# First attention of a fused layer chain: a new order of projections, maximum rows and value blocks, and inputs of the next batch loaded at other points

## What is computed

```
x = x + attention0(layernorm(x), ctx)     # 16 heads of 64, softmax(q k' / 8) v, then w_out
x = x + experts(layernorm(x))             # two of eight experts
x = x + attention1(layernorm(x), ctx)     # 16 heads of 16
x = x + quantised_ffn(layernorm(x))
```

```
q = layernorm(x) @ w_q;  k, v = split(ctx @ w_kv);  out = softmax(q @ k.T * 64**-0.5) @ v
```

## Time and profile before

| | |
|---|---|
| median of 3 runs | 3297.62 us |
| the profiled execution, its time | 3297.44 us |
| its span, first to last instruction | 3295.6 us |
| mean granted TensorE clock | 0.974 of full speed |
| TensorE matmul busy | 3098.3 us, 94% |
| VectorE busy | 2310.2 us, 70% |
| ScalarE busy | 1630.6 us, 49% |
| GpSimd busy | 1303.7 us, 40% |

### The profile page before, as it was taken

How to read it: one execution, slowest core, us unless ns; L and a number is a source line. 1 busy time by engine, 2 the same in 40 slices (tenths; PEclk the granted TensorE clock), 3 DMA queues, 4 the chain that set the end, 5 groups by cost and what they waited for, 6 DMA issues and landing times. The chain is left out here.

```text
span 3295.6 us, 40332 instructions
## 1 busy us (share of the span) xinstructions
PE 3098.3 (94%) x14204; PEld 1886.0 (57%) x14204; DVE 2310.2 (70%) x3680; ACT 1630.6 (49%) x1850; POOL 1303.7 (40%) x610
## 2 busy tenths in 40 slices
PE   6999999999999999999999969799999999999578
PEld 4556556556556566565565546455555555554368
DVE  5675785675775766757746524688888888888589
ACT  3443443443443434534534412366676576666388
POOL 1764774764765756747746723200000000000102
PEclk9999999999999999999999979799999999999798
DMA  8454553453553453544535332322322323222202
GB/s 219 112 124 110 128 139 89 114 146 85 126 147 83 106 144 99 123 123 107 125 102 121 78 106 80 83 44 65 73 50 66 67 49 72 66 49 59 72 13 90
DMA packets 182475, 317.40 MB, mean 96 GB/s; under 512 B 35081, under 2 KB 94289, under 8 KB 182289
## 3 DMA queue, kind: packets, MB, share of 16 engines
q1 hardware_dynamic: 182288, 315.00, 38.9%
HBM read 92.58 MB, written 29.36 MB: 37 GB/s over the span
## 5 line engine op out<-in xcount | busy, mean ns | idle before, releaser
L900 POOL TENSOR_TENSOR a_prob_sum<-a_prob_sum,a_prob 128x1024 f32<-128x1024 f32 x384 | 924.3, 2407 | 60.5 <-ACT a_prob L620 5.7
L620 ACT ACTIVATE a_prob<-a_t 128x1024 f32<-128x1024 f32 x512 | 516.6, 1025 | 660.5 <-PE a_t L445 472.7
L767 DVE TENSOR_REDUCE a_mhalves<-a_m 128x1 f32<-128x512 f32 x1024 | 690.2, 680 | 115.0 <-PE a_m L409 107.7
L1650 ACT ACTIVATE a_prob<-a_t 128x1024 f32<-128x1024 f32 x512 | 497.2, 1024 | 183.7 <-PE a_t L1491 182.8
L1747 DVE TENSOR_REDUCE a_mhalves<-a_m 128x1 f32<-128x512 f32 x807 | 537.5, 685 | 59.5 <-PE a_m L1470 55.2
L452 PE MATMUL a_o<-a_prob,a_v_all 128*64 128x512 f32 x2048 | 494.2, 605 | 0.0
L409 PE MATMUL a_m<-a_kh_n,a_qz 128*128 128x512 f32 x1024 | 415.0, 417 | 19.3 <-DVE a_kl_n L761 15.0
L900 POOL TENSOR_TENSOR a_prob_sum<-a_prob 128x1024 f32<-128x1024 f32 x64 | 153.3, 2395 | 575.0 <-ACT a_prob L620 511.8
L1470 PE MATMUL a_m<-a_vh,a_qz 128*128 128x512 f32 x807 | 335.7, 436 | 10.5 <-DVE x_sb L1819 4.5
L437 PE MATMUL a_t<-a_q_hl,a_k_hh 128*128 128x512 f32 x1024 | 324.1, 398 | 4.6 <-ACT a_prob L620 4.5
L445 PE MATMUL a_t<-a_q_hm,a_k_lm 66*128 66x512 f32 x1024 | 321.7, 395 | 0.0
(11 more groups left out here) (273 smaller groups left out, 4200.2 us busy)
## 6 DMA issues: line engine op xcount, KB each, us to landing
a_k_hh<-a_kh_n SPq DMA_DIRECT2D x256, 256.0 KB, 4.5
a_k_lm<-a_kl_n SPq DMA_DIRECT2D x128, 256.0 KB, 4.9
a_q_hl<-a_qz SPq DMA_DIRECT2D x128, 128.0 KB, 2.3
a_q_hm<-a_qz SPq DMA_DIRECT2D x128, 128.0 KB, 2.4
a_q_hl<-a_ql_n SPq DMA_DIRECT2D x128, 128.0 KB, 2.4
a_vs<-a_vh SPq DMA_DIRECT2D x256, 64.0 KB, 2.4
a_wq<-wq_parts SPq DMA_DIRECT2D x63, 256.0 KB, 2.7
a_wk<-wk_parts SPq DMA_DIRECT2D x63, 256.0 KB, 3.0
```

Of the source, the lines that this page charges most:

```text
L620: nc.scalar.activation(prob[:, t % RING], ps_t[t % 2][:, :, :], ACT.Exp, scale=SCALE0).then_inc(s_exp, 1)
L767: nc.vector.tensor_reduce(mhalves[:, qt, hd, n:n + 1], ps_m[:, n, :], AX.X, ALU.max).then_inc(s_max, 1)
L900: nc.gpsimd.tensor_tensor(acc, prob[:, (t - 1) % RING] if t == 1 else acc, prob[:, t % RING], ALU.add).then_inc(s_acc, 1)
L1650: nc.scalar.activation(prob[:, t % RB, 2 * j:2 * j + 2, :], ps_t[j][:, :, :], ACT.Exp, scale=SCALE1).then_inc(s_exp, 1)
```

## The change

In the first attention alone:
- On TensorE, `probs_v` of tiles 0 to 3 stand in one block (before: 0, 1, two maxima, 2, 3), and scores 5 come behind it. In p=7 scores 0 come ahead of the first maximum. The last two maxima come directly ahead of the values of tiles 4 and 5, and `max_rows` behind these values (in p=6, where the values 4 to 7 are one block, `max_rows` stays ahead of them).
- `project_k` comes ahead of `project_q`, and on ScalarE and VectorE the keys' splits ahead of the queries' (in p=6 queries stay first). The semaphores `s_kq`, `s_hi`, `s_lo` are split by keys and queries. SP's stacking starts with the keys.
- The reciprocals of the pair before stand ahead of maxima 7, 7, 8, 9 (before: 0, 9, 11, 12).
- The next rows are loaded straight into `xn`, as soon as the transposes have read it, and scaled in place, one row tile in each of p=1 to 4. The next context is loaded at the start of the batch, behind the storing of the context's parts.
- In p=6 VectorE subtracts the low transposed rows between the two parts of the context.

```diff
@@ block.sync, stack
+                sp.wait_ge(s_hk, nx.g + 1)
+                for hd in range(2):
+                    move(k_hh[heads[0], u, hd, :], kh_n[heads[hd], :])
+                    move(k_hh[heads[1], u, hd, :], kh_n[heads[hd], :])
+                sp.wait_ge(s_hq, 2 * nx.g + 2)
                 for hd in range(2):
                     move(q_hl[heads[0], u, hd, :], qz[heads[hd], hd, :])
                     move(q_hm[heads[0], u, hd, :], qz[heads[hd], hd, :])
...
@@ block.sync, batch
                 if not last:
 
-                    sp.wait_ge(s_cl, 2 * (b + 1))
-                    sp.dma_start(x_in[:], x_view[:, bass.ds((b + 1) * QT, QT), :]).then_inc(s_xin, 16)
+                    sp.wait_ge(s_tr, b + 1)
+                    sp.dma_start(xn[:], x_view[:, bass.ds((b + 1) * QT, QT), :]).then_inc(s_xin, 16)
...
+                if not last:
+                    load_context(b + 1)
                 stack(pair(b, 1), pair(b, 2))
...
-                if not last:
-
-                    sp.wait_ge(s_ln, 14 * (b + 2))
-                    load_context(b + 1)
                 stack(pair(b, NP - 1), None if last else pair(b + 1, 0))
@@ block.tensor, denominators and attend
                 if nn is not None:
-                    pe.wait_ge(s_lo, 3 * nn.g + 2)
+                    pe.wait_ge(s_lq, 2 * nn.g + 2)
...
+                elif pr.p == NP - 1:
+
+                    scores(pr, 0)
+                    maxima(1)
+                    scores(pr, 1, among())
+                    maxima(3)
                 else:
                     maxima(1)
-                    scores(pr, 0)
+                    scores(pr, 0, among())
                     maxima(1)
                     scores(pr, 1, among())
                     maxima(1)
                 scores(pr, 2, among())
                 maxima(1)
-                scores(pr, 3, among())
+                scores(pr, 3, among() if pr.p == 0 else None)
                 maxima(1)
                 scores(pr, 4, among())
-                if pr.p == 0:
-                    maxima(1)
-                scores(pr, 5, among())
-                maxima(1)
                 pe.wait_ge(s_oraw, pr.g)
                 probs_v(pr, 0)
                 probs_v(pr, 1)
-                maxima(2)
                 probs_v(pr, 2)
                 probs_v(pr, 3)
+                maxima(2)
+                scores(pr, 5, among() if pr.p == 0 else None)
                 maxima(1)
                 scores(pr, 6, among())
                 maxima(1)
-                if pr.p == 0:
-                    scores(pr, 7, among())
-                else:
-                    scores(pr, 7)
+                scores(pr, 7, among() if pr.p == 0 else None)
+                maxima(2)
                 assert not todo
-                if nx is not None:
+                if turned is not None:
+
                     max_rows(nx)
-                if turned is not None:
-
                     turn_queries(turned)
-                probs_v(pr, 4)
-                probs_v(pr, 5)
-                if turned is not None:
-
-                    probs_v(pr, KT - 2)
-                    probs_v(pr, KT - 1)
+                    for t in range(4, KT):
+                        probs_v(pr, t)
...
                 else:
+                    probs_v(pr, 4)
+                    probs_v(pr, 5)
+                    if nx is not None:
+                        max_rows(nx)
                     if nn is not None:
+                        project_k(nn)
                         project_q(nn)
-                        project_k(nn)
                     probs_v(pr, KT - 2)
                     probs_v(pr, KT - 1)
                 denominators(pr, nx, nn)
@@ block.scalar, attend
-                if nn is not None:
+                if turned is not None:
                     split_high_q(nn)
                     split_high_k(nn)
+                elif nn is not None:
+                    split_high_k(nn)
+                    split_high_q(nn)
                 keep_o(pr)
@@ block.vector, attend
-            INVERTED_AT = (0, 9, 11, 12)
+            INVERTED_AT = (7, 7, 8, 9)
...
                     split_context_low(split, 0)
+                    split_turned_low(split)
                     split_context_low(split, 1)
-                    split_turned_low(split)
...
                 if scaled is not None:
-                    scale_rows(nc, dve, rows, mv, rstd, xn, s_rstd, scaled + 1, s_ln)
-                if nn is not None:
-                    split_low(nn)
+
+                    b, qt = scaled
+                    dve.wait_ge(s_rstd, b + 1)
+                    nc.vector.tensor_scalar(xn[:, qt, :], xn[:, qt, :], mv[:, qt, 0:1], rstd[:, qt:qt + 1],
+                                            ALU.subtract, ALU.mult).then_inc(s_ln, 1)
+                if split is not None:
+                    split_low_q(nn)
+                    split_low_k(nn)
+                elif nn is not None:
+                    split_low_k(nn)
+                    split_low_q(nn)
```

More of the change, by code:

```diff
@@ L181, in first_attention @@
         s_vd = sem("v_kept_by_dve")
-        s_kq = sem("kq_projected")
-        s_hi = sem("kq_split_hi")
-        s_lo = sem("kq_split_lo")
+        s_kp = sem("keys_projected")
+        s_qp = sem("queries_projected")
+        s_hk = sem("keys_high")
+        s_hq = sem("queries_high")
+        s_lk = sem("keys_low")
+        s_lq = sem("queries_low")
         s_stk = sem("kq_stacked")
@@ L262, in stack @@
                     move(q_hm[heads[0], u, hd, :], qz[heads[hd], hd, :])
-                sp.wait_ge(s_lo, 3 * nx.g + 2)
+                sp.wait_ge(s_lk, nx.g + 1)
+                for hd in range(2):
+                    move(k_lm[heads[0], u, hd, :], kl_n[heads[hd], :])
+                sp.wait_ge(s_lq, 2 * nx.g + 2)
                 for hd in range(2):
                     move(q_hl[heads[1], u, hd, :], ql_n[heads[hd], :])
-                sp.wait_ge(s_hi, 3 * nx.g + 3)
-                for hd in range(2):
-                    move(k_hh[heads[0], u, hd, :], kh_n[heads[hd], :])
-                    move(k_hh[heads[1], u, hd, :], kh_n[heads[hd], :])
-                sp.wait_ge(s_lo, 3 * nx.g + 3)
-                for hd in range(2):
-                    move(k_lm[heads[0], u, hd, :], kl_n[heads[hd], :])
             def load_context(b):
@@ L370, in project_k @@
                     pe.wait_ge(s_zero, ZEROS)
+                else:
+                    pe.wait_ge(s_w[u], 32 * (pr.loads - 1 + u))
                 for n in range(2):
@@ L602, in _ @@
             max_rows(first)
+            project_k(pair(0, 1))
             project_q(pair(0, 1))
-            project_k(pair(0, 1))
             pe.wait_ge(s_const, 32)
@@ L623, in split_high_k @@
             def split_high_k(nx):
[L625 to L626 removed]
+                act.wait_ge(s_kp, 2 * nx.g + 2)
+                if nx.g:
+                    act.wait_ge(s_stk, STACKS * nx.g)
+                nc.scalar.copy(kh_n[:], ps_m[:].rearrange("p a n -> p (a n)")).then_inc(s_hk, 1)
             def split_high_q(nx):
[L630 removed]
+                act.wait_ge(s_qp, nx.g + 1)
                 if nx.g != 0:
@@ L635, in split_high_q @@
                     rows = slice(hd * HD0, (hd + 1) * HD0)
-                    nc.scalar.copy(qz[rows, hd, :], ps_x[rows, :]).then_inc(s_hi, 1)
+                    nc.scalar.copy(qz[rows, hd, :], ps_x[rows, :]).then_inc(s_hq, 1)
             def keep_max_rows(nx):
@@ L662, in attend @@
                         if t == 1:
-                            act.wait_ge(s_kq, 3 * NP * turned)
+                            act.wait_ge(s_kp, 2 * NP * turned)
                             act.wait_ge(s_cs, 48 * turned)
@@ L728, in _ @@
             keep_max_rows(first)
+            split_high_k(pair(0, 1))
             split_high_q(pair(0, 1))
-            split_high_k(pair(0, 1))
             for b in range(B):
@@ L735, in _ @@
         def _(dve):
-            rows = [x_in[:, qt, :] for qt in range(QT)]
+            rows = [xn[:, qt, :] for qt in range(QT)]
             first_rows = [x_res[:, qt, :] for qt in range(QT)]
@@ L819, in batch @@
                 for p in range(NP - 4):
-                    attend(pair(b, p), pair(b, p + 2), pair(b, p + 3))
-                attend(pair(b, NP - 4), pair(b, NP - 2), pair(b, NP - 1), scaled=None if last else b + 1)
+                    attend(pair(b, p), pair(b, p + 2), pair(b, p + 3), scaled=None if last else (b + 1, p))
+                attend(pair(b, NP - 4), pair(b, NP - 2), pair(b, NP - 1))
                 if last:
@@ L855, in _ @@
                 if t == KT // 2:
-                    split_low(first)
+                    split_low_q(first)
+                    split_low_k(first)
                 if t % 2:
@@ L861, in _ @@
             join_max(first)
-            split_low(pair(0, 1))
+            split_low_k(pair(0, 1))
+            split_low_q(pair(0, 1))
             for b in range(B):
```

31 lines of the change are left out of this document (15 added, 16 removed).

## The result

The changed kernel took 3291.79 us (median of 15 runs, 3288.88 to 3295.57), the kernel before 3298.83 us beside it (15 runs, 3296.85 to 3306.65). The ratio is 0.9976, with a 95% interval of 0.9968 to 0.9984: 7.0 us or 0.24% faster.

The account below looks back on a forecast made before the run. TensorE, busy 94% of the span, was taken as the bound. Terms +2.6 - 4.6 - 0.7 - 3.0 - 0.4 - 1.2 - 1.0 + 0.3 = -8.0 gave a median of 3289.6 us, range 3283 to 3296.

Parts of the forecast that it names:

- Step 1: Values of tiles 0 to 3 in one block: one less entry and exit of the 64-column form, -0.35 us per pair.
- Step 2: Maximum rows behind values of tiles 4 and 5: wait for VectorE's joined maxima goes, -0.22 us; order with keys adds nothing.
- Rival B: Maximum rows between 64-column values and 128-column keys cost up to 0.4 us in 55 pairs, 3311 us; chance 0.10.
- Step 3: Keys ahead of queries: denominators wait 0.59 us for the low queries and run 0.05 longer, +0.64 us per pair.
- Rival A: No wait at the denominators, low queries in time: 55 pairs lose 0.64 us, 3254 us; chance 0.12.
- Step 4: Row scalings spread over p=1 to 4, about 1.7 us each in VectorE's idle time; seven p=5 shorter, -4.6 us.
- Step 5: Turned pair (p=6, seven): old waits go, three new ones come; sum -0.1 us each, -0.7 in all.
- (a): In p=6, maximum rows directly behind two maxima: VectorE's reductions and join hold TensorE 1.45 instead of 0.22 us, +1.23.
- rival C: In p=6 the context tail misses its addition and waits 2.4 us more in seven batches, 3306 us; chance 0.08.
- Step 6: Context loaded most of a batch ahead: the one p=6 of 30.36 us falls to 27.34, -3.0 us.
- Step 7: p=7 and p=0: old waits go, crowded maxima and the denominators' wait come; -0.4 us for seven, -1.2 for eight.
- Step 8: Two ends: keys fill the query projection's wait before the first pair, -1.0 us; GpSimd's later additions in last p=6, +0.3.

Follow-up runs that it names:

- everything together: The changed kernel with the next pair's scores 0 ahead of the last values, spread maxima, and in p=7 the next batch's first value projection there: 3242.01 us, ratio 0.9825.

## Why the prediction was right, and where it was not

**Step 1, values in one block, -0.35.** Right; undone, it costs 0.38. The values are float32 and their neighbours float32r, so a change of data type is a rival for the form. In the turned pair the values follow float32 transposes of 128 columns, and entering the block costs 0.09 us there as it does behind float32r matmuls; leaving it stands in no such row, so that part isn't told apart.

**Step 2, maximum rows behind the values, -0.22 and nothing for the order with the keys.** Right. L378 follows L426 by 0.30 us, and its second matmul another 0.28 behind, 0.05 over the usual spacing. Rival B would have needed 0.27 or more; the 66-column matmul does not behave as the 64-column form does. With the measured 0.38 and 0.64 of steps 1 and 3, the pair's change from 24.51 to 24.53 leaves -0.24 for step 2, an estimate.

**Step 3, the wait for the low queries, 0.59 + 0.05.** Right in place, cause, count (55) and size: 0.58 measured, and 0.64 per pair given back when other work filled it. Rival A is wrong: the slack of 1.9 us was indeed eaten by the low keys in front and the six slots. What I failed to ask was how large the wait would be without the new order (1.39 us).

**The ordinary pair.** 24.53 on average against a forecast of 24.58; 33 pairs made +0.7 instead of +2.6. Of the 0.05 us per pair, 0.03 is the block (0.38 instead of 0.35); the rest stands in no single row.

**Step 4, scaling spread, -4.6.** Measured -5.1; the rest is the same 0.05 to 0.07 us per pair as in the ordinary ones. One thing in it was other than I had it, though it fell into idle time and cost nothing: one scaling at a time takes 0.4 us, not the 1.7 of my cover. All scalings of the changed kernel, and then of the kernel before (least, median and longest in ns):

```profile
L824 DVE TENSOR_SCALAR a_xn<-a_xn,a_mv,a_rstd x28: 402/405/684, 110.9 to 1583.6; 128x256 f32<-128x256 f32 x28
```

```profile
L84 DVE TENSOR_SCALAR a_xn<-a_ctx_raw,a_mv,a_rstd x28: 1075/1974/2624, 208.3 to 1621.2; 128x256 f32<-128x256 f32 x28
```

Their 28 instructions took 54 us before and 12 now, more than VectorE's whole fall. What makes them long is GpSimd's addition beside them, not their number and not the buffer. All 28 of the kernel before end 0.15 us behind the end of one of GpSimd's instructions, and the new ones are short because they fall at the end of one and are over as the next begins; three of the 28 start somewhat earlier, and take 0.64 to 0.68 us. Their place was luck: I had not asked where they would fall. Four in a row from another buffer are short too where GpSimd does nothing, at the start of the kernel before (first fence). So is the first of four, from the old buffer, in the run with the old loading, while the next two take 2.6 us each (second):

```profile
L84 DVE TENSOR_SCALAR a_xn<-a_x_res,a_mv,a_rstd x4: 407/407/414, 8.8 to 9.8; 128x256 f32<-128x256 f32 x4
```

```profile
L84 DVE TENSOR_SCALAR a_xn<-a_ctx_raw,a_mv,a_rstd x1: 404/404/404, 443.3 to 443.3; 128x256 f32<-128x256 f32 x1
```

The other way round, one small instruction of the rows' statistics, the same in both kernels, used to fall between two additions and now doesn't (before, then after):

```profile
L76 DVE TENSOR_SCALAR a_veps<-a_mv x7: 170/170/170, 87.6 to 1494.5; 128x4 f32<-128x4 f32 x7
```

```profile
L76 DVE TENSOR_SCALAR a_veps<-a_mv x7: 2274/2281/2308, 87.9 to 1487.1; 128x4 f32<-128x4 f32 x7
```

It costs VectorE 15 us and TensorE nothing, as VectorE is not the limit there. The Trainium skill, SBUF — State Buffer, SBUF: two separate sides, has a VectorE instruction in a two-port mode lock the port pair that it shares with GpSimd, or be locked out, for a whole instruction, and names tensor_scalar among those that can enter such a mode. The 0.17 and 2.28 us of one and the same instruction agree.

**Step 5, the turned pair, three waits in exchange for three.** Right in kind and near in size. (a) The rows' wait: 1.35 us of idle time, and by start times L426 is 1.51 us late where it was 0.22, so +1.29; forecast +1.23. (b) Scores 4 are held 0.34 us and the matmul after them starts 0.1 late, where the kernel before had 0.11 and 0.1, so +0.23; forecast +0.25. (c) The keys wait for the context tail by 0.33 us in all, forecast 0.5. Together 1.85 against my 1.98, with 2.03 gone: -0.2 per pair, and an undisturbed p=6 did go from 27.3 to 27.14. (My own terms add up to -0.05, which I had rounded to -0.1.) TensorE, then VectorE, in p=6 for the earlier trace rows:

```profile
467.27 0.47 PE L426 MATMUL a_x<-ident,a_mcol 128*66 128x128 f32 x4 [1.35 <-DVE a_mcol L788]
...
472.15 0.50 PE L398 MATMUL a_x<-a_xnT,a_wq 128*128 128x512 f32 x1
...
473.88 0.50 PE L378 MATMUL a_m<-a_ctx_high,a_wk 128*128 128x512 f32 x1
```

```profile
467.14 3.38 DVE L756 TENSOR_TENSOR a_ctx_low<-a_ctx_raw,a_ctx_high 128x1024 fp32r<-128x1024 f32 x1
470.44 1.21 DVE L761 TENSOR_TENSOR a_xnT_low<-a_m,a_xnT 128x1024 fp32r<-128x1024 f32 x1
471.68 2.14 DVE L756 TENSOR_TENSOR a_ctx_tail<-a_ctx_raw,a_ctx_tail 64x1024 fp32r<-64x1024 f32 x1
```

L398 has no wait any more, as forecast. The tail takes 2.14 us and ends at 473.82, just ahead of L378: it doesn't miss its addition, and rival C is wrong. Now the context's low part bears the stretch, 3.38 us.

**Step 6, context in time, -3.0.** Wrong in size, and the one step where I read the profile badly. The 30.36 us pair stood in one batch of seven of one execution. There TensorE stood idle behind the late cast and then had the lower clock level, 1.2 GHz, from 695.8 us on for 3.4 us, which its own idle time may have brought on:

```profile
694.34 0.73 PE L437 MATMUL a_t<-a_q_hl,a_k_hh 128*128 128x512 f32 x2 [2.08 <-ACT a_prob L620]
```

The second profile of before has no such pair. I took the difference of one outlier to its neighbour (whose mean clock was 1.00, against 0.94) for the price of an order. p=6 as a whole fell by 4.8 us against the profile that I read but by 2.6 against the second. If 27.30 us, its shortest p=6, is what a pair takes with the context in time, the seven of the second profile stand 1.4 us over that together, and those of the first 3.7: in an execution without the outlier the step is worth 1.4 us (an estimate), not 3. That a late context costs something is borne out by the waits in 9 of 14 batches.

**Step 7, p=7 and p=0.** p=7: three maxima in a row cost what I said, one short wait at maximum 0 (0.38 us) and then 0.25 and 0.46; measured -0.9 for seven, forecast -0.4. p=0: the sign was wrong, +1.8 instead of -1.2. I had 0.25 for maxima 13 to 15 being too close. But maximum 9 is too close to the one before it on its bank as well. TensorE in p=0 around maxima 8 and 9, and around the last ones:

```profile
545.61 0.74 PE L413 MATMUL a_m<-a_kh_n,a_qz 128*128 128x512 f32 x2
546.19 0.63 PE L441 MATMUL a_t<-a_q_hl,a_k_hh 128*128 128x512 f32 x2
546.90 0.50 PE L413 MATMUL a_m<-a_kh_n,a_qz 128*128 128x512 f32 x1
...
550.51 0.98 PE L413 MATMUL a_m<-a_kh_n,a_qz 128*128 128x512 f32 x2
551.42 1.08 PE L456 MATMUL a_o<-a_prob,a_v_all 128*64 128x512 f32 x4
```

Two scores matmuls from 546.19 to 546.90 are 0.71 us for 0.47 of work, so 0.24 of wait, and the matmul after the maximum comes 0.34 behind it instead of 0.23. The last two maxima take 0.91 us to the values, from 550.51, where those of an ordinary pair take 0.56 (from 391.30): 0.35. Together 0.69, nearly three times my 0.25. With 0.38 and 0.69 gone and 0.64 for the denominators that makes +0.26 per p=0, as measured. Spreading the maxima took 0.35 per p=0 off.

**Step 8, the ends.** The last p=6 +0.3 as forecast. The last p=7 was the second miss, +1.6 instead of 0. Its start:

```profile
1871.24 1.08 PE L472 MATMUL a_x<-a_prob_sum,ones 128*64 128x512 f32 x4 [2.45 <-POOL a_prob_sum L923]
1872.25 1.18 PE L441 MATMUL a_t<-a_q_hl,a_k_hh 128*128 128x512 f32 x2
...
1879.18 0.62 PE L441 MATMUL a_t<-a_q_hl,a_k_hh 128*128 128x512 f32 x2
```

I had counted that GpSimd's additions end this p=6 later, and TensorE is idle 2.45 us for them (1.90 in the kernel before). I had not counted what followed: TensorE is granted the lower of its clock levels (1.2 GHz) from 1872.3 on for 6.8 us, in which a group of two matmuls takes 1.05 to 1.18 us instead of 0.62. In this pair GpSimd's chain of additions is the limit. It begins 5.9 us behind the pair's start, as its exponentials are late, where it began 4.3 behind it in the kernel before, and then runs without a pause in both: that is the 1.6 us. The fall came in five of the twelve profiled executions: the changed kernel both times, and those with two blocks, early scores 0 and low queries first. It did not come in the kernel before, both times, nor with queries first, old loading, spread maxima, rows ahead or everything together; there the pair took 21.82 to 21.84 us. The length of the idle time alone doesn't decide it: it came behind 1.98 us (scores 0 early) and 2.05 us (two blocks), and did not behind 2.41 us (old loading), 2.43 us (queries first) and 2.45 us (spread maxima). What does is not settled, and so neither is whether this 1.5 us belongs to the change.

So the mechanism was right where most of the pairs are, in steps 1 to 4 (ordinary pairs and p=5), whose sum was -2.0 and measured -4.4. That the sum came within 1 us (-7.1 in the profiles against -8.0) is partly luck. Step 6 put 3.0 of the 8.0 us on one outlier of one profile. And errors cancel: p=0 and the last pair came out 4.6 us worse than forecast, the ordinary pairs, p=5, p=6 and p=7 together 4.0 us better, 2.2 of it from p=6 of the first profile of before, where the outlier stands.

## What to carry to other kernels

When projections, splits and the end of an iteration are a chain over three engines, ask of each order how far the last link stands from the iteration's end, and look for work of the next iteration that is ready to stand between: that was worth 35 us here, five times the change itself, some 30 of it the wait. Where a tensor is double-buffered and another engine empties it, list the distance of every use to the one before it on its bank, also in the few odd iterations; close ones cost the wait and 0.1 us at the matmul behind it. Where one engine's instructions have several lengths, look what another does beside them before a length goes into a sum. A single long iteration in one profile is a sample, not a term: look for its like in the other batches and take a second profile before it goes into a sum.

## What the runs showed of the hardware that I had not expected

- VectorE's scaling of 128x256 took 0.40 us where none of GpSimd's additions stood in its way, in place or from another buffer, alone or as one of four, and up to 2.62 us beside them, each ending 0.15 us behind the end of one of GpSimd's instructions. A scaling of 128x4 took 0.17 us between two additions and 2.28 beside one.
- Among 128-column float32r matmuls one entering and leaving of a block of 64-column float32 ones cost 0.38 us here. A 66-column matmul ahead of 128-column ones cost 0.05.
- Where TensorE waited for VectorE's read of a bank, the matmul behind the one that waited came 0.34 us after it instead of 0.23. In twelve executions no maximum of the first attention started less than 1.17 us behind the one before it on its bank.
- In the last pair of the first attention TensorE's clock stood at its lower level (1.2 GHz) for 6.8 and 3.4 us in the two executions of the changed kernel, and not in the two of the kernel before. Over twelve executions it came five times, behind idle times of 1.98 to 2.48 us, and stayed away seven times, behind 1.16 to 2.45. In the kernel before it came once elsewhere, for 3.4 us, shortly behind 2.08 us of idle time.
